# A Macaron layer on one core: stack loads issued by ScalarE, six fills and one set of statistics moved, and a new placement of the side work

## What is computed

```python
x = x + 0.5 * ffn(layernorm(x), W1, b1, W2, b2)    # relu(x @ Q(W1).T + b1) @ Q(W2).T + b2
x = x + attn(layernorm(x), Wq, bq, Wk, bk, Wv, bv, Wo, bo)
x = x + 0.5 * ffn(layernorm(x), W1, b1, W2, b2)

# attn
q, k = rope(q, k)
scores = einsum("bhnd,bhmd->bhnm", q, k) / sqrt(8)
out = einsum("bhnm,bhmd->bhnd", softmax(scores), v)
return out @ Wo.T + bo
```

## Time and profile before

| | |
|---|---|
| median of 3 runs | 550.92 us (543.98, 550.92, 551.0) |
| the profiled execution | 548.73 us |
| its span, first to last instruction | 546.6 us |
| PE, DVE, ACT, POOL busy | 498.3, 392.0, 369.1, 213.8 us |
| mean granted TensorE clock | 0.975 |
| phase 0 (e1 to the next phase's e1) | 69.6 to 135.7 us |
| phases 1 to 6 start at | 135.7, 193.5, 251.2, 308.2, 367.7, 425.5 us |
| phase 7 | from 479.8 us |

### The profile page before, as it was taken

One profiled execution on the slowest core, in us unless ns is written; L12 is line 12 of the kernel. 1 busy time (PEld: TensorE's weight loads), 2 busy tenths in 40 slices (PEclk: granted clock), 3 DMA queues, 4 the chain that ended last, 5 costly groups with the idle time before them and its releaser, 6 DMA issues.

```text
span 546.6 us, 12209 instructions
## 1 busy us (share of the span) xinstructions
PE 498.3 (91%) x4981; PEld 233.6 (43%) x4981; DVE 392.0 (72%) x582; ACT 369.1 (68%) x440; POOL 213.8 (39%) x286
## 2 busy tenths in 40 slices
PE   7887869979999999999999996999799988999986
PEld 5654523432453435353535332433234333433445
DVE  4578558766888688778787884868767886788324
ACT  2767457885858685867676764777576767667751
POOL 3315057336454283447351744145612731103202
PEclk9999779998999999999999997999989999999999
DMA  8054015602370129003620344024701380000000
GB/s 272 8 203 106 1 27 192 134 2 73 122 157 3 42 98 229 7 26 113 181 55 22 118 135 101 2 60 156 156 2 41 123 208 3 22 2 3 3 20 20
DMA packets 18967, 44.44 MB, mean 81 GB/s; under 512 B 2400, under 2 KB 5472, under 8 KB 17888
## 3 DMA queue, kind: packets, MB, share of 16 engines
q1 hardware_dynamic: 18240, 43.14, 28.5%
q10 hardware_dynamic: 672, 0.52, 0.3%
HBM read 20.58 MB, written 18.87 MB: 72 GB/s over the span
## 4 chain that ended last, share of the span: by engine, by line
PE 69%; ACT 10%; DVE 6%; issue 4%; DMA 4%; POOL 2%; SPq 0%; ACTq 0%; POOLq 0%; DVEq 0%
PE heads_acc L565 22%; PE unit L550 14%; PE unit L535 11%; PE side L629 8%; ACT probs L767 7%; DMA q_stack<-max_T 4%; DVE maxima L874 3%; PE side L604 3%; PE side L621 2%; ACT hidden L757 2%; PE side L614 2%; PE side L599 2%; PE side L584 1%; PE side L589 1%; ACT heads L773 1%
## 5 line engine op out<-in xcount | busy, mean ns | idle before, releaser
L874 DVE TENSOR_REDUCE maxima<-unit 128x2 f32<-128x1024 f32 x256 | 304.4, 1221 | 89.5 <-PE unit L535 88.5
L767 ACT ACTIVATE probs<-unit 128x1024 f32<-128x1024 f32 x256 | 255.8, 1023 | 100.9 <-PE unit L550 99.8
L565 PE MATMUL heads_acc<-probs,v_heads 128*32 128x512 f32 x1024 | 137.9, 611 | 0.9 <-ACT probs L767 0.9
L550 PE MATMUL unit<-q_stack,k_stack 64*128 64x512 f32 x512 | 116.1, 469 | 22.6 <-DMA q_stack<-max_T 11.6
L535 PE MATMUL unit<-k_stack,q_stack 62*128 62x512 f32 x512 | 108.7, 444 | 4.3 <-ACT probs L767 2.4
L550 PEld LDWEIGHTS unit<-q_stack,k_stack 64*128 64x128 f32 x512 | 47.4, 186 | 100.1 <-ACT probs L767 39.6
L1067 POOL TENSOR_SCALAR max_parts<-maxima 128x16 fp32r<-128x16 f32 x32 | 6.5, 204 | 182.0 <-DVE maxima L874 182.0
L535 PEld LDWEIGHTS unit<-k_stack,q_stack 62*128 62x128 f32 x512 | 48.9, 190 | 59.4 <-issue 22.6
L629 PE MATMUL side<-w_q,hidden 128*32 128x128 f32 (+1 forms) x1472 | 53.9, 276 | 2.7 <-ACT hidden L757 2.7
L629 PEld LDWEIGHTS side<-w_q,hidden 128*32 128x32 f32 (+1 forms) x1472 | 46.0, 114 | 13.3 <-issue 10.5
L565 PEld LDWEIGHTS heads_acc<-probs,v_heads 128*32 128x32 f32 x1024 | 21.9, 108 | 37.0 <-issue 30.1
(11 more groups left out here) (160 smaller groups left out, 464.3 us busy)
## 6 DMA issues: line engine op xcount, KB each, us to landing
k_scratch<-k_parts SPq DMA_DIRECT2D x16, 512.0 KB, 3.4
q_scratch<-q_parts SPq DMA_DIRECT2D x16, 512.0 KB, 3.4
k_stack<-k_scratch SPq DMA_DIRECT2D x14, 512.0 KB, 7.1
q_stack<-q_scratch SPq DMA_DIRECT2D x14, 512.0 KB, 9.2
resid<-in_x SPq DMA_DIRECT2D x8, 256.0 KB, 5.2
k_swap<-k SPq DMA_DIRECT2D x14, 128.0 KB, 2.3
q_swap<-q SPq DMA_DIRECT2D x14, 128.0 KB, 2.3
out_y<-resid SPq DMA_DIRECT2D x7, 256.0 KB, 2.1
```

Of the source, the lines that this page charges most:

```text
L550: mm = pe.matmul(to[:, e, :], k_stack[part, quad // NQ % 2, pair, kt * P:(kt + 1) * P], q_stack[part, quad // NQ % 2, pair, :], start=True ...
L565: mm = pe.matmul(heads_acc[32 * j:32 * j + 32, :], v_heads[:, b % 2, at, ODD * odd:ODD * odd + 32], probs[:, burst % RING, j, :], start=(k ...
L767: act.activation(probs[:, burst % RING, 2 * pp:2 * pp + 2, :], unit_of(USE_OF["exp", n]), ACT.Exp, scale=SCALE).then_inc(s_exp, 1)
L874: dve.tensor_reduce(maxima[:, quad % 2, :, r], unit_of(USE_OF["max", k]), AX_X, ALU.max).then_inc(s_max, 1)
```

## The change

Five edits:

1. The stack load of batches 1 to 7 is no longer issued by SP but by ScalarE, on ScalarE's own DMA queue, at a new token `stack`, with the same waits. The load of batch 0 stays with SP. SP's list for a phase now goes from the q parts' copies straight to the row pair of quad 2.
2. Of the eight fills of the second slot two (was: four) stand in the stretch before phase 0; six are tokens rows0 to rows5 of phase 0.
3. In phase 0 the statistics of batch 5 (ffn1_stats@5) move from ahead of e1 to behind e12.
4. Phase 0's other tokens stand elsewhere.
5. In phases 1 to 7 many tokens move by one or a few places.

```diff
-AHEAD = {"ffn1": 4, "attn": 2, "k": 2, "q": 2, "v": 1, "out": -1, "ffn2": -1}
+AHEAD = {"ffn1": 4, "attn": 2, "k": 2, "q": 2, "v": 1, "out": -1, "ffn2": -1, "stack": 1}
...
+ROWS_LATE = [(0, "k", 1), (0, "q", 1), (1, "k", 0), (1, "k", 1), (1, "q", 0), (1, "q", 1)]
...
                 if on("values", b):
                     to_scratch("q", b + 1)
-                    stack(b + 1, slice(0, NPAIR), s_stack[(b + 1) % 2])
...
+            def stack(j):
+                for n in "qk":
+                    act.wait_ge(s_scratch[n], (j + 1) * 16 * PARTS)
+                wait(act, s_scoresT, (j - 1) * STEPS)
+                for e in range(2):
+                    for n, tile in (("k", k_stack), ("q", q_stack)):
+                        products = scratch[n][j % 2].rearrange("q k (d e h) t -> (q k d) e (h t)", d=DH, e=2)
+                        act.dma_start(tile[64 * e:64 * e + PROD, j % 2, :, :].bitcast(F32).rearrange("p h t -> p (h t)"),
+                                     products[:, e, 0:NPAIR * S]).then_inc(s_stack[j % 2], 16)
...
                 if k in (2, 3):
                     set_rows(1, 0, "kq"[k - 2], 0)
-                if k in (7, 8):
-                    set_rows(1, 0, "kq"[k - 7], 1)
...
                 elif use[0] == "rows":
-                    set_rows(1, 1, "kkqq"[use[1]], use[1] % 2)
+                    set_rows(1, *ROWS_LATE[use[1]])
+                elif use[0] == "stack":
+                    stack(use[2])
```

The stretch of the steady table around the row pair of quad 2, before and after:

```diff
-e m m ffn1_down2 ffn1_down3
-e m pv m
-e pv attn_stats max_T2 m
-e
-e v pv m ffn2_T
-e pv m
+e ffn1_down2 m
+e m ffn1_down3 pv stack m attn_stats
+e pv max_T2 m
 e
+e v pv m
+e ffn2_T
```

More of the change, by code:

```diff
@@ L49 @@
 LATE_CONST_DMAS = 4
-AHEAD = {"ffn1": 4, "attn": 2, "k": 2, "q": 2, "v": 1, "out": -1, "ffn2": -1}
+AHEAD = {"ffn1": 4, "attn": 2, "k": 2, "q": 2, "v": 1, "out": -1, "ffn2": -1, "stack": 1}
 PE_FIRST = """
-attn_T@1 ffn1_stats@5 e
+e attn_T@1 m
 e m k@1 m
-e
-e m q@1
-e m ffn1_T m pv m
-e ffn1_up0 m max_T1
-e m ffn1_up1 m m rows0 ffn1_up2 pv m m pv
+e m q@1 m ffn1_T
+e m m
+e max_T1
+e m m ffn1_up0 rows0 m
+e ffn1_up1 m pv ffn1_up2
+e pv
 e m ffn1_up3
 e
-e ffn1_down0
-e m
-e ffn1_down1 ffn1_down2 rows3 rows2 m ffn1_down3 pv attn_stats
-e
-e pv
-e m pv m max_T2 pv m
-e m rows1 m pv
-heads_copy0 e m v
-e
-e
-e attn_T m pv m
-e
-e pv m max_T3
-e heads_T0
-e m
-e
-e
-e m
-e m pv k m m pv q
-e m
-e max_T4 pv m
-e pv
-e m pv
+e ffn1_down0 m
+e ffn1_stats@5 rows1 m ffn1_down1 stack rows3 rows2 ffn1_down2 ffn1_down3 m m
+e max_T2 pv pv
+e m pv m attn_stats pv m rows5
+e pv
+e v rows4
+e m
+heads_copy0 e pv
+e heads_T0 m
+e attn_T m
+e m
+e max_T3
+e m pv m m pv
+e
+e pv m
+e pv m
+e
+e pv k
+e m
+e pv max_T4 m
+e m q m pv
+e
 """
@@ L92 @@
 m ffn1_T e m pv
-heads_copy1@-1 ffn1_up0 e m ffn1_up1
-e m heads_T1@-1
-e m
-e pv ffn1_up2
-e m ffn1_stats@5 pv max_T1
-e m m out_T pv ffn1_up3 m
-e out
-e
-e m pv ffn1_down0
-e ffn1_down1 ffn2_stats
-e m m ffn1_down2 ffn1_down3
-e m pv m
-e pv attn_stats max_T2 m
-e
-e v pv m ffn2_T
-e pv m
-heads_copy0 e m ffn2_up0
-e m ffn2_up1
-e pv heads_T0
-e m m ffn2_up2
+heads_copy1@-1 ffn1_up0 e m ffn1_up1 m
+e heads_T1@-1
+e
+e m pv ffn1_up2
+e m ffn1_stats@5 m max_T1 pv
+e m out_T pv ffn1_up3 m
+e out
+e m
+e pv ffn1_down0
+e ffn2_stats m ffn1_down1
+e ffn1_down2 m
+e m ffn1_down3 pv stack m attn_stats
+e pv max_T2 m
+e
+e v pv m
+e ffn2_T
+heads_copy0 pv e m ffn2_up0
+e m m ffn2_up1 pv heads_T0
+e m ffn2_up2
+e m
 e pv max_T3
 e m m ffn2_up3 pv
-e m ffn2_down0 m m
-e ffn2_down1 ffn2_down2 ffn2_down3
-e m
-e pv attn_T
-e
-e m k pv
-e m m max_T4 pv
+e m ffn2_down0 m
+e m ffn2_down1 ffn2_down2
+e m
+e ffn2_down3 pv attn_T
+e m
+e pv k
+e m m pv max_T4
 e m q
@@ L574, in side_work @@
                 name, arg, index, b = use
-                if name in ("heads_copy", "rows", "ffn1_stats", "attn_stats", "ffn2_stats"):
+                if name in ("heads_copy", "rows", "stack", "ffn1_stats", "attn_stats", "ffn2_stats"):
                     return
```

## The result

The changed kernel took 573.2 us (median; 572.7 to 574.1) where the kernel before took 549.4 us beside it (544.0 to 551.0): a ratio of 1.045, interval 1.037 to 1.053. It is slower, and of the cases in the prediction it is the one called "no passing at all" (580 us). All rows of "after" are from an execution with a span of 570.6 us, 24.0 us longer than the one of before.

What follows compares the result with a forecast made beforehand. The prediction took TensorE to bound phases 1 to 3, with slack in phases 0 and 4 to 6, mainly waits for row pairs behind the load. Sum: 548.7 - 8 - 13.4 + 10.5 = 538 us; range 529 to 559.

Steps and rivals of the forecast that it cites:

- no passing at all: Rival, phases 1 to 6: small transfers end with the load, waits of 7 to 8 us; 580 us; chance 0.12.
- Phase 0 and the stretch before it: Term for the kernel's start: 9.6 us gained, 1.5 for moved fills, 3 lost on ScalarE; 8 us gained.
- The stall for statistics: Start of phase 0: VectorE's wait for GpSimd over the second statistics would go; 3.8 us gained.
- the 2.9 us of half clock: Phase 0, 75 to 82 us: the half clock would go with the statistics stall; up to 2.9 us gained.
- the moved pieces: Stretch before phase 0: two fills leave it for phase 0; 1.5 us gained.
- The rival in which ScalarE waits at its queue's head: Phase 0: ScalarE arrives before the scratch copies land; up to 4 us lost, 542 us; chance 0.1, within the main case.
- What ScalarE pays: Phases 4 to 6: four DMA issues take 1.8 us, making e14 0.9 us and max_T 0.7 us late.
- What it brings near: Phases 1 to 6: row pair meets the load; new waits 1.4 us in phases 1 to 3, 2.1 in 4 to 6; 10.5 us.
- turns packet by packet: Shared transfer engines: queues alternate by packets, so the load holds up the row pair by 0.6 to 1.9 us, taken as 1.6.
- The first rule that the prediction took from the Trainium skill: Issuing engines share the same 16 DMA engines; a second issuer saves only issue time; read strictly, 580 us.
- The old waits: Phases 4 to 6: row-pair waits of 10.4 us and about 3 us of half clock would go; 13.4 us gained.
- my signs of being wrong: Phases 1 to 3 pair waits over 3 us; maxima waiting for load; ScalarE idle before DMA issues; phase 0 over 61 us.

Runs made afterwards that it cites:

- e1: First of a phase's 32 exponentials; as a run, the changed kernel with the load back on SP, behind the q parts' copies; 548.5 us.
- e12: 12th exponential of a phase; as a run, the kernel of e10 with phases 4 to 6's load halved around quad 2's row pair, on SP; 525.0 us.
- e9: The kernel before, with SP issuing the row pair of quad 2 ahead of the load in phases 4 to 6; 550.4 us, ratio 1.002.
- e2: The changed kernel, with ScalarE issuing the load four exponentials earlier, behind the ninth, in phases 1 to 7; 537.5 us.
- e6: The changed kernel, with the load issued behind the 11th exponential instead of e13 in phases 1 to 7; 552.1 us.
- e14: Not a run: the 14th of the 32 exponentials that run in a phase.
- e13: Not a run: the 13th of the 32 exponentials of a phase; in phases 1 to 7 the changed kernel issues the load behind it.
- e3: The changed kernel, with gaps between scratch rows so that the load is made of 2 KB packets instead of 16 KB ones; 571.5 us.
- e8: The kernel of e1, with ScalarE issuing all 32 row pairs on its own queue while the load stays on SP; 561.2 us.
- e5: The changed kernel, with ScalarE issuing two load transfers behind e13 and two behind e15 in phases 1 to 7; 562.3 us.
- e11: The kernel of e5, with the second half of the load issued behind the 16th exponential instead of e15; 532.5 us.
- e17: Not a run: the 17th of the 32 exponentials of a phase; it needs the row pair of quad 2.
- e7: The kernel of e1, with SP's load in phase 0 held back until the 12th exponential is done; 540.9 us.
- e4: The kernel before, with only the new table of phase 0 and the new places of the fills, load on SP; 545.3 us.
- e15: Not a run: the 15th of the 32 exponentials that run in a phase.
- e10: The kernel of e7, with the row pair of quad 2 issued ahead of the load in phases 4 to 6; 537.6 us.

## Why the prediction was wrong

**Phase 0 and the stretch before it: the sum was right, by luck.** I had 8 us and the two traces give 8.3. Phase 0 is 4.5 us shorter, where I had 6.6 (9.6 less 3). The stall for statistics is gone (0.68 us in place of 3.77), but the 2.9 us of half clock behind it, which I had counted as gone, are not: a wait of 1.56 us for GpSimd came in its place and the clock is at 0.53 from 75 to 82. The half clock at 122.9 is gone, and TensorE waits 0.27 us for the pair of quad 2 and 1.1 us for an exponential. In phase 0 ScalarE has 50.9 us of work, 3.8 more, as worked out.

The other 3.7 us stand before e1, where I had given the moved pieces 1.5. From the first max_T to the scores of e1 before takes 10.4 us and after 6.7. e9, which has the code of before there, takes 8.5, since it has one stretch of half clock less than before. So 1.8 us are the moved pieces, near my 1.5, and 1.9 us are a half clock that this one execution of before had. The wait for the hidden tile in e9 and in after:

```profile
58.89 1.13 PE L633 MATMUL side<-w_q,hidden 128*128 128x128 f32 x8 [1.31 <-ACT hidden L761]
```

```profile
59.70 1.13 PE L629 MATMUL side<-w_q,hidden 128*128 128x128 f32 x8 [0.33 <-ACT hidden L757]
```

The rival in which ScalarE waits at its queue's head did not come in phase 0; e2 and e6 show that it does in phases 4 to 6, if the load is moved forward.

**What ScalarE pays: mis-sized, to nothing.** I had e14 0.9 us late in phases 4 to 6. In phase 4 e13 starts at 338.64 and e14 at 340.51, 1.87 us later, exactly as before (325.52 and 327.39). The issues begin 0.1 us behind e13's start, not behind its end, and are over at 340.46, when TensorE's scores for e14 have just come (340.43).

**What it brings near: the step that failed.** "How two queues share the transfer engines no row of before shows" was true. I then took 1.6 us from a place between the bounds, by a picture of turns packet by packet, and gave the upper bound, the rest of the load, a chance of 0.12. The upper bound is what happens. The six waits are 36.6 us where I had 10.5. e3 takes the picture away: with packets of 2 KB the waits are shorter by 0.1 to 0.8 us. e8 shows the same with the queues exchanged, and e5 shows the order itself. By the Trainium skill, "DMA: Bandwidth & Descriptors", section "Queues, rings and completion order", each DMA engine alternates between queues by packets; the traces here disagree (0 of 177 packets in 10 us, 0 of 591 in e3), and the measurement decides. That page's packet is a bundle of descriptors, typically 9 to 17, and a row of the trace need not be one. But in e5 a turn was at most 42 of the load's 128 large packets, and with such turns the pair of the changed kernel would have been read before 288.4. Section "Issuing engines are not separate DMA queues" of that page says that a second issuer saves issue time only, and the runs agree with it: e12, with all on SP's queue, is rid of nearly all the waits (525.0 us), e11, with the load on ScalarE's, takes 532.5, and what brought the 36.6 us was the place of the load, since e2 has the same queue without them.

I had the row that should have weighed more. In phase 4 of before the small pair ended with the load; I explained that by the shared queue, which no row proved. The neutral reading was that 16 KB behind 2.1 MB take 12.9 us, and that the change puts the pair 3 to 4 us behind the load in six phases, where before it was 5 to 7 us behind it in three. The first rule that the prediction took from the Trainium skill pointed that way.

**The old waits.** 13.4 us were to be gained in phases 4 to 6. The mechanism was right (e12 has it), but in the changed kernel the new waits replace the old ones and the half clock stays.

**The rival's price.** 580 us was near, 7 us too high: its waits were to be 7 to 8 us and are 5.4 to 6.6, since e17 is due 7.0 us behind the load's first issue in phase 3 (284.8 less 277.8) and 6.1 in phase 4, not 5 to 6. The point from which it decides, 3.6 us per phase, held: 6.1 us per phase made it slower. Of my signs of being wrong two came: waits over 3 us in phases 1 to 3, and a phase 0 longer than 61 us (61.6).

**The sum again.** Phases 1 to 6 were to lose 13.4 and gain 10.5, -2.9 us; they gained 32.0. Of the 34.9 us between, 26.1 are the size of the new waits, and 8.8 what I had counted as 3 us of clock won back and is 5.8 us of clock and small waits lost (in these phases TensorE is busy 6.6 us more for the same work, and idle 25.4 us more).

**What stays open.** Whether the small transfer waits inside the DMA engines, or before them where the transfers are cut into packets, no row tells: a trace shows packets when they are read. In e6 and e11 SP's second issue of a pair took up to 2.8 us in place of 0.6, and that is not explained either. The 8 us that e7 is better than the kernel before lie ahead of phase 1 (3.6 before e1, partly half clock as said above, and 4.4 in phase 0); its phases 1 to 6 are 0.8 us longer. Whether the halves around the pair would bring e12's gain in phases 4 to 6 with the old steady table, too, was not run.

## What to carry to other kernels

A second queue is not a second lane. Before moving a transfer to another queue, list what is issued ahead of each small transfer that an engine waits for, on all queues together, code fetches too, as far back as the largest transfer lasts (here 10 us); if something large is there, issue it earlier, or cut it and put the small one between. And if a price is not in the trace and its upper bound is already to be seen on another path (here: 12.9 us for a pair behind a load), take the bound as the first guess, until something shows that the new path differs.

When a transfer is moved out of one wait, look up who reads it next (e9): a wait of 10.4 us turned into one of 9.8.

## What the runs showed of the hardware beyond that

- Transfers of two queues ran in one line by time of issue: a pair of 8 KB transfers issued 4.1 us behind a 2.1 MB load on the other queue was read 10.6 us behind the load's first issue with packets of 16 KB; with packets of 2 KB it was issued 4.4 us behind and read 10.3.
- A load can hold up instruction packets as well: with the load issued 3 us earlier, a 16 KB packet of instructions was read about 5 us later (94 in place of 89 us) and TensorE stood for 4.67 us (3.70 in e4, 4.78 in e8); holding the load back 4.4 us took it away and gave 7.6 us. By the Trainium skill, "Runtime: NRT & Kernel Launch", section "Instruction fetch mechanics", the refill of instructions by DMA is mostly hidden; in e1, e4 and e8 it was not.
- ScalarE issued DMAs beside a running activation, but the next activation came behind the last issue: in phase 4 four issues took 1.7 us and e14 was not late. In phase 3 they took 2.75 us (277.81 to 280.56); e14 started at 280.61, 0.2 us later than in e1 (2.90 us behind e13 in place of 2.71), and e15 had made that up.
- Half clock behind waits cost about as much again as the waits. In phases 4 to 6 of e12 TensorE is idle 6.9 us less than in e10, and busy 7.2 us less for the same work, at a clock of 1.00 throughout. The waits for stacks and pairs are 6.9 us shorter (2.4 for 9.3), and the kernel 12.6 us.
